# Third layer's heads: two key blocks' value products in a row, score passes interleaved

## The chip, the core and the metric

The kernel runs on one core of a Trainium2 chip. The metric is the device time of one execution in microseconds (us). The core's engines run unsynchronised, each with its own queue: TensorE multiplies matrices (PE in the profile, its weight loads PEld), VectorE (DVE), ScalarE (ACT) and GpSimd (POOL) work on elements, and SyncE (SP) here only issues transfers. Semaphores order them: an instruction adds to one when it is done, and another engine's `wait_ge` holds its queue until the value is there.

## What is computed

Four layers in turn, each `x = x + attention(norm(x)) + feed_forward(norm(x))`, on x of 2 sequences, 1024 tokens and 256 features. The change lies in the third layer's attention (called L2, counted from 0), 16 heads of 16 features:

```
q, k, v = (split_heads(q), split_heads(k), split_heads(v))   # (2, 16, 1024, 16)
scores = jnp.einsum('bhqd,bhkd->bhqk', q, k) * scale
attn = jnp.einsum('bhqk,bhkd->bhqd', jax.nn.softmax(scores, axis=-1), v)
g = jax.nn.sigmoid(gate)
combined = g * mem_out + (1.0 - g) * attn
```

## The kernel before

`l2_heads` computes `attn` in 32 steps, one for each pair (h, b) of head and sequence; step n is n = 2h + b. Steps 0, 1, 30 and 31 are written out, those between are a hardware loop (`steps`, L1565). For each pair the work on TensorE comes in three kinds:

- First pass (`first_pass`, L1647, matmul L1658). Scores with queries on partitions, in NP = 16 pieces of 128 queries by 512 keys. Its only use is the maximum of each row. Piece i goes into PSUM buffer `s1[i % 2]`, and before it is written TensorE waits on `maxed` until VectorE has reduced piece i - 2 (L1657). VectorE does one `reduce_max` of 128x512 for each piece (`maxima`, L1747), and after 16 pieces a small `take_top` (L1752).
- Second pass (`second_pass`, L1661, matmul L1668). Scores with keys on partitions, for one key block kb of 8: two matmuls of 128x512 into `s2[kb % 2]`. The row maxima are subtracted through two extra rows of the contraction. TensorE waits on `exped` until ScalarE has done key block kb - 2; ScalarE takes the exponential of all 1024 queries in one instruction (L1734) into `PT`.
- Value products (`values`, L1672, matmul L1680). For one key block four matmuls of 256 queries each, with a stationary operand 32 columns wide, put side by side in the four column groups of the array (their outputs are the partition groups 0-31, 32-63, 64-95 and 96-127 of `pv`). Each float32 matmul has two records in the trace, so a key block shows as eight.

A fourth piece, `turn` (L1684), comes once a step: it transposes the finished `ctxT` of an earlier step (two transposes, not in steps 0 and 1) and the row maxima `top` of the next one (L1695), and counts up `turned`. On VectorE `split_max` (L1754) waits for it, makes `mhi` and `mlo` (L1758, L1760), and `normalise` (L1762, two instructions, not in steps 0 and 1) follows. SyncE then carries `mhi` and `mlo` into `Q2` (`load_max`, L1615) for the second pass of the next step.

The work is staggered: in step n TensorE does the second pass of n, the first pass of n + 2, and the value products of n - 1. The order is written out by hand in `step` (L1702): for each kb, two second-pass matmuls, two first-pass pieces, at kb == TURN_AT (1) the `turn`, then the value products of kb. VectorE's order (`step`, L1778) is: maxima of pieces 0 to 2 * (TURN_AT + 1) - 1, `split_max`, `normalise`, the other maxima, `take_top`. So TURN_AT sets both TensorE's place for the turn and how many maxima VectorE does ahead of waiting for it.

Step 0 has no value products, and steps 30 and 31 have no first pass. After step 31 the value products of the last pair run as eight key blocks in a row.

Of the kernel before, what the change touches and what calls it, by code (L numbers as in the profile page):

```python
# [21 lines left out]
NQ = S // P  # L22
# [54 lines left out]
def wait(engine, sem, value):  # L77

    if not isinstance(value, int) or value > 0:
        engine.wait_ge(sem, value)  # L80
# [1229 lines left out]
def l2_attn(nc, k, a):  # L1310

    split = nc.dram_tensor("l2_split", [2, 4, D, T], F32, kind="Internal").ap()
    with Stage(nc, "l2a") as st:
        VA = st.sb("VA", [P, TT, L2_HEADS, L2_W])
        mem = st.sb("mem", [P, DC, T])
        gate = st.sb("gate", [P, 2, DC])
        with Stage(nc, "l2q") as s2:
            QF = s2.sb("QF", [P, DC, T])  # L1320
            KF = s2.sb("KF", [P, DC, T])
            hi, lo = s2.sb("hi", [P, 2, DC, BANK], F32R), s2.sb("lo", [P, 2, DC, BANK], F32R)
            hi_stored, lo_stored = [s2.sem(f"hi_stored{i}") for i in range(2)], [s2.sem(f"lo_stored{i}") for i in range(2)]
            l2_project(nc, k, a, split, VA, QF, KF, hi, lo, hi_stored, lo_stored)
            l2_memory(nc, k, a, VA, QF, KF, mem, gate, hi_stored + lo_stored)
        CT = st.sb("CT", [P, TT, D])
        l2_heads(nc, k, split, VA, CT)
        l2_output(nc, k, a, CT, mem, gate)
# [210 lines left out]
def l2_heads(nc, k, split, VA, CT):  # L1539
# [4 lines left out]
    with Stage(nc, "l2h") as st:  # L1544
# [17 lines left out]
        pv_made, pv_kept, turned, inv_ready, ctx_kept = (st.sem(n) for n in ("pv_made", "pv_kept", "turned", "inv_ready", "ctx_kept"))  # L1562
        vh_ready, second_loads = st.sem("vh_ready"), st.sem("second_loads")
        NP = 2 * NQ
        TURN_AT = 1  # L1565
        MROW = SPLIT

        def steps(engine, step):

            for b in range(B):  # L1570
                step(0, b)
            with engine.Fori(1, L2_HEADS - 1) as h:
                for b in range(B):
                    step(h, b)
            for b in range(B):
                step(L2_HEADS - 1, b)

        def after(h, b, n):

            return (h + (b + n) // B, (b + n) % B)  # L1580

        def before(h, b):
            return (h, b - 1) if b else (h - 1, B - 1)

        def is_first(h, b):
            return isinstance(h, int) and h == 0 and b == 0

        def exists(h, b, n):

            return not isinstance(h, int) or B * h + b + n < L2_N  # L1590

        with nc.Block() as block:
# [56 lines left out]
            @block.tensor  # L1649
            def _(pe):  # L1650
                def first_pass(h, b, pieces):
                    n = B * h + b
                    for i in pieces:
                        t, z = divmod(i, 2)
                        if i == 0:
                            pe.wait_ge(q1_loaded[b], 32 * h + 32)
                        wait(pe, maxed, NP * n + i - 1)  # L1657
                        pe.matmul(s1[i % 2][:, :], Q1[:, b, t * P:(t + 1) * P], K1[:, b, z * BANK:(z + 1) * BANK],  # L1658
                                  start=True, stop=True).then_inc(s1_made, 1)

                def second_pass(h, b, kb):  # L1661
                    n = B * h + b
                    if kb == 0:
                        pe.wait_ge(q2_loaded[b], 32 * h + 32)
                        pe.wait_ge(m_loaded[b], 32 * h + 32)
                    wait(pe, exped, NQ * n + kb - 1)
                    for z in range(NZ):
                        mm = pe.matmul(s2[kb % 2][:, z * BANK:(z + 1) * BANK], K2[:, b, kb * P:(kb + 1) * P],  # L1668
                                       Q2[:, b, z * BANK:(z + 1) * BANK], start=True, stop=True)
                    mm.then_inc(s2_made, 1)  # L1670

                def values(h, b, kb):  # L1672

                    n = B * h + b
                    if kb == 0:
                        pe.wait_ge(vh_ready, n + 1)
                        pe.wait_ge(exped, NQ * (n + 1))
                        wait(pe, pv_kept, n)
                    for g in range(4):
                        mm = pe.matmul(pv[g * L2_W:(g + 1) * L2_W, 0:2 * P], VH[:, b, kb, :],  # L1680
                                       PT[:, b, kb, g * 2 * P:(g + 1) * 2 * P], start=(kb == 0), stop=(kb == NQ - 1), skip_group_check=True)
                    if kb == NQ - 1:
                        mm.then_inc(pv_made, 1)

                def turn(m, ctx, top_of):

                    wait(pe, m_ready, min(m, L2_N) if isinstance(m, int) else m)
                    if ctx:
                        pe.wait_ge(pv_kept, m - 2)
                        wait(pe, ctx_kept, m - 3)  # L1690
                        for i in range(2):
                            mm = pe.transpose(turns[:, i * P:(i + 1) * P], ctxT[:, i * P:(i + 1) * P], k.ident[:, :])
                    if top_of is not None:
                        pe.wait_ge(top_ready, m + 1)
                        mm = pe.transpose(pmt, top[:, top_of, :], k.ident[:, :])  # L1695
                    mm.then_inc(turned, 1)

                first_pass(0, 0, range(NP))
                turn(0, False, 0)
                first_pass(0, 1, range(NP))  # L1700

                def step(h, b):  # L1702
                    for kb in range(NQ):
                        second_pass(h, b, kb)
                        if exists(h, b, 2):
                            first_pass(*after(h, b, 2), range(2 * kb, 2 * kb + 2))
                        if kb == TURN_AT:
                            turn(B * h + b + 1, not isinstance(h, int) or h > 0, (b + 1) % B if exists(h, b, 1) else None)
                        if not is_first(h, b):
                            values(*before(h, b), kb)  # L1710

                steps(pe, step)
                turn(L2_N + 1, True, None)
                for kb in range(NQ):
                    values(L2_HEADS - 1, B - 1, kb)
                turn(L2_N + 2, True, None)
# [24 lines left out]
            def _(dve):  # L1741
# [36 lines left out]
                def step(h, b):  # L1778
                    n = B * h + b
                    more = exists(h, b, 2)  # L1780
                    early = 2 * (TURN_AT + 1)
                    if more:
# [995 lines left out]
```

## Time and profile before

| | |
|---|---|
| Time, median of 3 runs | 4075.12 us (4071.56 to 4076.61) |
| Profiled execution | 4091.38 us, span 4089.6 us |
| Span of this stage's heads in it | 2301.2 to 2773.6 us, 472 us |
| Mean granted TensorE clock | 0.929 |
| Busy share: PE, PEld, DVE, ACT, POOL | 89%, 65%, 57%, 39%, 34% |

The whole program has one execution in the trace. What matters for this change is a stretch of 12% of it, in which one step repeats. The trace rows give start and duration of instructions. A matmul's record runs from when its data are first fetched to a modelled end, so the records of neighbours overlap, and their starts tell the pace. A matmul whose weights could be loaded ahead has a record of 0.39 to 0.40 us at full clock; one that had to wait for its weights has one of about 0.50 us, and its data stream some 0.1 us after its record begins.

### The profile page before, as it was taken

How to read it: one execution, taken by the hardware profiler on the slowest of the kernel's cores; microseconds unless marked ns; L12 is line 12 of the kernel's file. 1: busy time of each engine (PE TensorE's matmuls, PEld its weight loads, DVE VectorE, ACT ScalarE, POOL GpSimd, SP SyncE). 2: the span in 40 equal slices, each digit the busy share in tenths (PEclk: the TensorE clock that was granted, in tenths of full speed). 3: DMA queues.
4: the chain of work that ended last, by engine and by line, in shares of the span. 5: the costliest groups of instructions: out<-in, count | busy, mean ns of one | idle time of the engine just before them, and what ended most of it. 6: DMA issues, size and time to landing. Idle time of an engine off the chain costs nothing. (4 is left out here: it accounts for less than half of the span.)

```text
span 4089.6 us, 65022 instructions
## 1 busy us (share of the span) xinstructions
PE 3655.6 (89%) x21096; PEld 2662.2 (65%) x21096; DVE 2325.4 (57%) x4783; ACT 1598.5 (39%) x2884; POOL 1389.7 (34%) x1087
## 2 busy tenths in 40 slices
PE   6999999999797999999966799997899979999676
PEld 4777777777575888888833344443678737776354
DVE  3555555555325566666647778774566646666444
ACT  2444444444233444444423166662333333333211
POOL 1333333333135666666614000000223352334254
PEclk8999999999898999999978799998899989999755
DMA  0000000000001000000004122210333313332144
GB/s 35 5 5 5 3 5 5 5 3 5 32 0 45 18 17 20 18 17 17 8 3 183 42 74 76 76 65 26 83 82 87 90 34 76 91 82 54 57 103 95
DMA packets 115990, 178.66 MB, mean 44 GB/s; under 512 B 22288, under 2 KB 65040, under 8 KB 115600
## 3 DMA queue, kind: packets, MB, share of 16 engines
q1 hardware_dynamic: 109776, 169.38, 13.8%
q0 software_dynamic: 6144, 8.39, 1.3%
q8 instruction: 38, 0.62, 0.1%
q14 instruction: 32, 0.26, 0.0%
HBM read 151.51 MB, written 25.95 MB: 43 GB/s over the span
## 5 line engine op out<-in xcount | busy, mean ns | idle before, releaser
L424 POOL TENSOR_TENSOR l0h_probs<-l0h_probs,l0h_inv 128x128 f32<-128x128 f32 (+7 forms) x256 | 292.8, 1146 | 585.7 <-DVE l0h_inv L459 585.7
L1747 DVE TENSOR_REDUCE l2h_half<-l2h_s 128x1 f32<-128x512 f32 x512 | 329.6, 685 | 94.2 <-PE l2h_s L1658 94.1
L1734 ACT ACTIVATE l2h_PT<-l2h_s 128x1024 f32<-128x1024 f32 x256 | 261.9, 1023 | 194.2 <-PE l2h_s L1668 194.2
L355 PE MATMUL l0h_sc<-l0a_KT,l0h_QT 128*128 x768 | 296.7, 499 | 30.0 <-ACT l0h_probs L528 28.3
L382 PE MATMUL l0h_cx<-l0h_PT,l0h_VG 128*128 128x128 f32 x2304 | 300.7, 276 | 0.0
L528 ACT ACTIVATE l0h_probs<-l0h_sc,l0h_negtop 128x128 f32<-128x128 f32 (+7 forms) x256 | 189.6, 741 | 245.4 <-DVE l0h_negtop L454 245.0
L382 PEld LDWEIGHTS l0h_cx<-l0h_PT,l0h_VG 128*128 128x128 f32 x2304 | 278.0, 192 | 1.1
L159 POOL TENSOR_TENSOR XN<-XN,n_rstd 128x512 f32<-128x512 f32 x32 | 39.8, 1265 | 635.2 <-DVE n_rstd L140 635.2
L2189 DVE TENSOR_TENSOR_SCAN l3p_table<-l3p_decb,l3p_eye 128x512 f32<-128x512 f32 x128 | 149.8, 1212 | 116.0 <-DMA l3p_prow<-l_decays 92.2
L1658 PE MATMUL l2h_s<-l2h_K,l2h_Q 128*128 128x512 f32 x512 | 180.2, 429 | 21.7 <-DMA l2h_K<-l_split 18.0
L452 DVE TENSOR_REDUCE l0h_top<-l0h_sc 128x1 f32<-128x128 f32 (+7 forms) x256 | 194.0, 758 | 8.8
L355 PEld LDWEIGHTS l0h_sc<-l0a_KT,l0h_QT 128*128 128x128 f32 x768 | 125.5, 192 | 106.7 <-issue 63.9
L1668 PE MATMUL l2h_s<-l2h_Q,l2h_K 128*128 128x512 f32 x512 | 187.5, 447 | 0.1
L391 PE MATMUL l0h_outp<-l0h_ctxT,l0h_wd 128*128 128x128 f32 x1024 | 163.8, 283 | 24.8 <-ACT l0h_ctxT L521 11.7
L369 PEld LDWEIGHTS l0h_tp<-ident,l0h_probs 128*128 128x128 f32 x1152 | 138.6, 141 | 64.3 <-issue 39.6
L2157 POOL TENSOR_TENSOR l3p_w_lo<-l3p_w,l3p_w_hi 128x1024 fp32r<-128x1024 f32 x34 | 80.3, 2362 | 276.8 <-ACT l3p_w_hi L2111 276.8
L2147 POOL TENSOR_TENSOR l3a_Y<-l3p_skip,l3p_sz 128x512 f32 (+1 forms) x64 | 81.4, 1272 | 261.6 <-DVE l3p_skip L2180 261.6
L369 PE MATMUL l0h_tp<-ident,l0h_probs 128*128 128x128 f32 x1152 | 168.7, 274 | 0.0
L470 DVE COPY l0h_PT<-l0h_tp 128x256 f32<-128x256 f32 (+2 forms) x192 | 98.6, 514 | 114.2 <-PE l0h_tp L369 112.3
L391 PEld LDWEIGHTS l0h_outp<-l0h_ctxT,l0h_wd 128*128 128x128 f32 x1024 | 134.2, 191 | 44.6 <-ACT l0h_ctxT L521 31.2
L514 ACT ACTIVATE l0h_PT<-l0h_tp 128x512 f32<-128x512 f32 (+1 forms) x192 | 100.8, 525 | 159.5 <-PE l0h_tp L369 159.1
L1680 PE MATMUL l2h_pv<-l2h_PT,l2h_VH 128*32 128x256 f32 x2048 | 162.1, 391 | 0.2 <-ACT l2h_ctxT L1725 0.2
(410 smaller groups left out, 9081.1 us busy)
## 6 DMA issues: line engine op xcount, KB each, us to landing
l3p_decb<-l_decays SPq DMA_DIRECT2D x128, 256.0 KB, 5.2
l3p_w<-L_w SPq DMA_DIRECT2D x34, 512.0 KB, 5.9
l2h_Q<-l_split SPq DMA_DIRECT2D x64, 256.0 KB
l2h_K<-l_split SPq DMA_DIRECT2D x64, 256.0 KB
l3p_prow<-l_decays SPq DMA_DIRECT2D x128, 128.0 KB, 5.6
l_split<-l2q_hi SPq DMA_DIRECT2D x16, 512.0 KB, 4.0
l_split<-l2q_lo SPq DMA_DIRECT2D x16, 512.0 KB, 3.8
mx_wgu<-L_ffn_w_gate_up SPq DMA_DIRECT2D x32, 256.0 KB
```

The lines of the kernel that those rows point to most:

```text
L355: mm = pe.matmul(sc[u % 2][:, lo:lo + n], QT[:, u * P:(u + 1) * P], KT[:, ds(g, 1), b * S + lo:b * S + lo + n], start=True, stop=True)
L369: mm = pe.transpose(tp[n % 2][:, (kb - q) * P:(kb - q + 1) * P], probs[:, u % 4, kb * P:(kb + 1) * P], k.ident[:, :])
L382: mm = pe.matmul(cx[:, 0:P], VG[:, b * NQ + kb, :], PT[:, u % 2, kb, :], start=(kb == 0), stop=(kb == t))
L391: mm = pe.matmul(outp[:, c * P:(c + 1) * P], wd[:, c * P:(c + 1) * P], ctxT[:, u % 2, :], start=True, stop=True)
L424: pool.tensor_tensor(p, p, inv[:, u % 4:u % 4 + 1].to_broadcast([P, keys(u)]), ALU.mult).then_inc(probs_scaled, 1)
L452: dve.reduce_max(top[:, u % 2:u % 2 + 1], sc[u % 2][:, 0:keys(u)], AX_X).then_inc(top_ready, 1)
L528: act.activation(probs[:, u % 4, 0:keys(u)], sc[u % 2][:, 0:keys(u)], ACT.Exp, bias=negtop[:, u % 2:u % 2 + 1], scale=L0_SCALE, accum_out= ...
L1658: pe.matmul(s1[i % 2][:, :], Q1[:, b, t * P:(t + 1) * P], K1[:, b, z * BANK:(z + 1) * BANK], start=True, stop=True).then_inc(s1_made, 1)
L1668: mm = pe.matmul(s2[kb % 2][:, z * BANK:(z + 1) * BANK], K2[:, b, kb * P:(kb + 1) * P], Q2[:, b, z * BANK:(z + 1) * BANK], start=True, sto ...
L1680: mm = pe.matmul(pv[g * L2_W:(g + 1) * L2_W, 0:2 * P], VH[:, b, kb, :], PT[:, b, kb, g * 2 * P:(g + 1) * 2 * P], start=(kb == 0), stop=(kb ...
L1734: act.activation(PT[:, b, kb, :], s2[kb % 2][:, :], ACT.Exp, scale=L2_SCALE).then_inc(exped, 1)
L1747: dve.reduce_max(half[:, b, t, z:z + 1], s1[i % 2][:, :], AX_X).then_inc(maxed, 1)
```

## The change

In `step` of TensorE the loop runs over pairs of key blocks (kb = 0, 2, 4, 6). For each pair: piece 2kb of the first pass, the second pass of kb, piece 2kb + 1, the second pass of kb + 1, pieces 2kb + 2 and 2kb + 3, the turn where kb is TURN_AT, and then the value products of kb and kb + 1 in a row. TURN_AT goes from 1 to 2, so the turn comes after piece 7, and VectorE does maxima 0 to 5 ahead of it. No instruction is added or removed. Buffers, waits, transfers and the code of the other engines stay as they are.

```diff
-        TURN_AT = 1
+        TURN_AT = 2
@@ step of TensorE
-                    for kb in range(NQ):
-                        second_pass(h, b, kb)
+                    for kb in range(0, NQ, 2):
+                        for i in range(2):
+                            if exists(h, b, 2):
+                                first_pass(*after(h, b, 2), (2 * kb + i,))
+                            second_pass(h, b, kb + i)
                         if exists(h, b, 2):
-                            first_pass(*after(h, b, 2), range(2 * kb, 2 * kb + 2))
+                            first_pass(*after(h, b, 2), (2 * kb + 2, 2 * kb + 3))
                         if kb == TURN_AT:
                             turn(B * h + b + 1, not isinstance(h, int) or h > 0, (b + 1) % B if exists(h, b, 1) else None)
                         if not is_first(h, b):
-                            values(*before(h, b), kb)
+                            for i in range(2):
+                                values(*before(h, b), kb + i)
```

## Rows read from the trace of the kernel before

**Rows 1.** The page: TensorE's busy share, and VectorE's group of maxima.

```profile
PE 3655.6 (89%) x21096; PEld 2662.2 (65%) x21096; DVE 2325.4 (57%) x4783; ACT 1598.5 (39%) x2884; POOL 1389.7 (34%) x1087
...
L1747 DVE TENSOR_REDUCE l2h_half<-l2h_s 128x1 f32<-128x512 f32 x512 | 329.6, 685 | 94.2 <-PE l2h_s L1658 94.1
```

**Rows 2.** Busy time by stretch: ramp, step 0, steps 1-29, steps 30-31.

```profile
core 0: us, PE busy (x) PEld busy (x) DVE busy (x) ACT busy (x) POOL busy (x), PEclk, DMA share, GB/s
2301.20:2326.99 25.79, 21.80 (x34) 9.34 (x35) 20.33 (x34) 0.00 (x0) 0.00 (x0) 0.50 0.18 66
2328.50:2339.40 10.90, 10.22 (x33) 5.55 (x32) 10.42 (x18) 8.03 (x9) 0.00 (x0) 0.93 0.17 66
2339.40:2748.00 408.60, 408.44 (x2873) 200.62 (x2876) 326.39 (x609) 254.60 (x291) 0.00 (x0) 1.00 0.20 74
2748.00:2773.20 25.20, 23.64 (x229) 9.70 (x228) 1.99 (x9) 17.50 (x21) 0.00 (x0) 1.00 0.07 22
```

**Rows 3.** Timeline, one key block; start us, us, engine, line, xcount, [idle before].

```profile
2503.79 0.64 PE L1680 MATMUL l2h_pv<-l2h_PT,l2h_VH 128*32 128x256 f32 x8
2504.36 0.30 PEld L1668 LDWEIGHTS l2h_s<-l2h_Q,l2h_K 128*128 128x128 f32 x2 [0.41 <-issue]
2504.36 0.74 PE L1668 MATMUL l2h_s<-l2h_Q,l2h_K 128*128 128x512 f32 x2
...
2504.94 0.63 PE L1658 MATMUL l2h_s<-l2h_K,l2h_Q 128*128 128x512 f32 x2
2505.13 1.02 ACT L1734 ACTIVATE l2h_PT<-l2h_s 128x1024 f32<-128x1024 f32 x1 [0.68 <-PE l2h_s L1668]
2505.37 0.69 DVE L1747 TENSOR_REDUCE l2h_half<-l2h_s 128x1 f32<-128x512 f32 x1 [0.41 <-PE l2h_s L1658]
...
2505.49 0.64 PE L1680 MATMUL l2h_pv<-l2h_PT,l2h_VH 128*32 128x256 f32 x8
```

**Rows 4.** Timeline, ScalarE's first exponential of steps 2 and 29.

```profile
2353.48 1.01 ACT L1734 ACTIVATE l2h_PT<-l2h_s 128x1024 f32<-128x1024 f32 x1
...
2733.97 1.02 ACT L1734 ACTIVATE l2h_PT<-l2h_s 128x1024 f32<-128x1024 f32 x1
```

**Rows 5.** Timeline, PE and DVE, around one turn and the two blocks behind.

```profile
2510.04 0.62 PE L1658 MATMUL l2h_s<-l2h_K,l2h_Q 128*128 128x512 f32 x2
...
2510.72 0.27 PE L1695 MATMUL l2h_turns<-ident,l2h_top 128*8 128x128 f32 x1
...
2510.92 0.64 PE L1680 MATMUL l2h_pv<-l2h_PT,l2h_VH 128*32 128x256 f32 x8
...
2511.67 0.27 DVE L1758 CAST l2h_mhi<-l2h_turns 8x128 fp32r<-8x128 f32 x1
...
2512.51 0.29 DVE L1769 TENSOR_TENSOR l2a_CT<-l2h_turns,l2h_inv 128x128 f32 x1
...
2512.72 1.28 DVE L1747 TENSOR_REDUCE l2h_half<-l2h_s 128x1 f32<-128x512 f32 x2
...
2513.75 0.81 PE L1658 MATMUL l2h_s<-l2h_K,l2h_Q 128*128 128x512 f32 x2
...
2514.05 0.19 PEld L1658 LDWEIGHTS l2h_s<-l2h_K,l2h_Q 128*128 128x128 f32 x1 [0.34 <-DVE l2h_half L1747]
...
2514.49 0.64 PE L1680 MATMUL l2h_pv<-l2h_PT,l2h_VH 128*32 128x256 f32 x8
```

**Rows 6.** Timeline, last value products: eight key blocks in a row.

```profile
2769.10 3.66 PE L1680 MATMUL l2h_pv<-l2h_PT,l2h_VH 128*32 128x256 f32 x64
```

**Rows 7.** Timeline of step 0, no value products: the split, then first and second pass.

```profile
2331.42 0.27 DVE L1758 CAST l2h_mhi<-l2h_turns 8x128 fp32r<-8x128 f32 x1
...
2331.93 0.67 DVE L1747 TENSOR_REDUCE l2h_half<-l2h_s 128x1 f32<-128x512 f32 x1
...
2334.25 1.02 ACT L1734 ACTIVATE l2h_PT<-l2h_s 128x1024 f32<-128x1024 f32 x1 [0.68 <-PE l2h_s L1668]
2334.53 0.19 PEld L1658 LDWEIGHTS l2h_s<-l2h_K,l2h_Q 128*128 128x128 f32 x1 [0.41 <-DVE l2h_half L1747]
...
2335.54 1.03 ACT L1734 ACTIVATE l2h_PT<-l2h_s 128x1024 f32<-128x1024 f32 x1 [0.26 <-PE l2h_s L1668]
```

**Rows 8.** Timeline of step 30, no first pass: end of the turn, then exponentials.

```profile
2749.26 0.27 PE L1695 MATMUL l2h_turns<-ident,l2h_top 128*8 128x128 f32 x1
...
2749.57 0.28 DVE L1758 CAST l2h_mhi<-l2h_turns 8x128 fp32r<-8x128 f32 x1 [1.54 <-PE l2h_turns L1695]
...
2752.03 1.02 ACT L1734 ACTIVATE l2h_PT<-l2h_s 128x1024 f32<-128x1024 f32 x1 [0.21 <-PE l2h_s L1668]
...
2753.26 1.02 ACT L1734 ACTIVATE l2h_PT<-l2h_s 128x1024 f32<-128x1024 f32 x1 [0.21 <-PE l2h_s L1668]
```

**Rows 9.** SyncE's waits in steps 1 to 29: us in total, times, longest us.

```profile
SPq L1608 <- PE l2h_s L1668: 195.1, 28, 7.2
SPq L1615 <- DVE l2h_mlo L1760: 59.0, 28, 3.0
```

## The prediction

> **What bounds the kernel now.** I read the page first: TensorE is busy 89% of the span, but VectorE's largest group of instructions, the maxima of this stage, stands there too [rows 1]. Then the stage alone, by stretch. In steps 1 to 29 TensorE is busy 408.4 of 408.6 us at full clock (1.00, which is 2.4 GHz), VectorE 326.4 and ScalarE 254.6 [rows 2]. So TensorE sets the pace on average, with VectorE at 80% behind it. The busy time of TensorE is made of overlapping records, so the pace must be read from starts.
>
> One key block [rows 3]: the value products start at 2503.79, the second pass at 2504.36, the first pass at 2504.94, the next value products at 2505.49: 1.70 us. Its parts:
> - value products, up to the weight load of the second pass: 0.57;
> - from that load to the second matmul of the pair: 0.74 less a record of 0.40 = 0.34. Where weights were loaded ahead, matmuls start 0.63 - 0.40 = 0.23 apart (0.24 where the operands change), so 0.10 of the 0.34 is an exposed load;
> - second matmul to first piece 0.24, to second piece 0.23;
> - last piece (2504.94 + 0.23 = 2505.17) to the value products at 2505.49: 0.32, where the next score matmul would have come after 0.23.
>
> Sum 0.57 + 0.34 + 0.47 + 0.32 = 1.70. The stream of four groups side by side needs about 0.43 for a key block: eight in a row take 3.66 from first start to last end, one takes 0.64, and (3.66 - 0.64) / 7 = 0.43 [rows 6]. So a visit to the value products costs 0.57 + 0.10 + 0.09 = 0.76, and each further key block in the same visit 0.43.
>
> A step, from the first exponentials of steps 2 and 29, is (2733.97 - 2353.48) / 27 = 14.09 us [rows 4]. Eight times 1.70 is 13.60. The turn adds 0.33: from the last piece (2510.04 + 0.23 = 2510.27) to the value products at 2510.92 it is 0.65 in place of 0.32 [rows 5]. The last 0.16 is the one wait on VectorE that TensorE feels: the two pieces of kb = 3 take 0.81 in place of 0.62, the load between them released by a maximum, because VectorE came late from the split [rows 5].
>
> **The change, part by part.**
>
> *Value products in pairs.* One visit fewer in each pair: 0.76 - 0.43 = 0.33 us saved. Without any new wait a pair would take 2 x 1.70 - 0.33 = 3.07 us. What stands against it is not in that sum: the order of the score passes.
>
> *First-pass pieces closer together.* There are two s1 buffers, so piece i + 2 waits for the maximum of piece i. The round trip: start of a piece to its maximum 2505.37 - 2504.94 = 0.43 [rows 3]; the maximum 0.69 (mean 0.685) [rows 1]; its end to the released weight load 2514.05 - (2512.72 + 1.28) = 0.05; and that load is exposed, 0.12, since the value products come 0.44 after it and not 0.32 [rows 5]. Sum 1.29 us. Step 0, which has no value products, shows it directly: exponentials 2335.54 - 2334.25 = 1.29 apart, with the piece's load waiting on the maxima [rows 7]. Before, pieces i and i + 2 are a key block, 1.70, apart, so it is hidden. In the new order (call the pieces of a pair F0 to F3) it is F0 S S F1 S S F2 F3 V V. F0 to F2 is six spacings, 1.41: hidden. F1 to F3 is four spacings, 0.24 + 0.23 + 0.24 + 0.23 = 0.94: F3 waits 1.29 - 0.94 = 0.35 us in every pair. F2 to the next F0 is over 2 us: hidden. VectorE is not behind from elsewhere: F3's maximum ends 0.43 + 0.69 = 1.12 after F3 starts, and the value products take TensorE 0.32 + 1.00 + 0.10 = 1.42 to the next F0. So a pair takes 3.07 + 0.35 = 3.42 us, against 3.40: the wait eats what the pairing saves. Bounds for the wait: 0.33 to 0.36 by the spread of the same rows (round trip 1.28 to 1.29, spacing 0.93 to 0.95).
>
> *The turn after piece 7, and six maxima ahead of it.* Before, VectorE is still at a maximum when the turn is done (2510.72 + 0.27 = 2510.99) and starts the split at 2511.67, with no idle time [rows 5]. After, VectorE has done maximum 5 when piece 7 is allowed to start (that is what piece 7 waits for), so it idles until the turn is done, and maxima 6 and 7 queue behind split and normalise though their scores are there. From the start of piece 7: turn done 0.45 + 0.27 = 0.72; split starts 0.04 later (2749.57 against 2749.26 + 0.27) [rows 8]; split and normalise hold VectorE 2512.72 - 2511.67 = 1.05 [rows 5]; maximum 6 takes 0.69; release 0.05. Piece 8 can load at 0.76 + 1.05 + 0.69 + 0.05 = 2.55 us. TensorE gets to it after the turn 0.65 and two key blocks of value products 0.57 + 0.43: at 1.65 us. The wait is 0.90 us once a step, bounds 0.85 to 0.95. It replaces the 0.16 of before. Behind it everything on TensorE is queued; piece 9 no longer waits, since maximum 7 ends 0.6 after maximum 6.
>
> *Work moved past other queues.* SyncE's `load_max` waits for the split, now about 3 us later in the step. SyncE waits there 59 us in 28 steps now, and 195 us (up to 7.2 each) at the next second-pass load, L1608 [rows 9]: the later start comes out of that. The `mhi` and `mlo` are wanted at the next step, some 8 us after the split. ScalarE gets two exponentials closer together: second-pass pairs are 0.70 apart, an exponential takes 1.02 [rows 3], both fit into 3.42 us and `s2` has two buffers, free again a pair later. Cost nothing, while ScalarE's 2.05 of 3.42 holds.
>
> *A step:* 4 x 3.42 + 0.33 + 0.90 = 14.91 us, against 14.09: + 0.82. For steps 2 to 29: 28 x 0.82 = + 23.0.
> *Edges.* Step 1 has value products but neither normalise nor the ctxT transposes: the split starts 0.23 + 0.27 + 0.04 = 0.54 after piece 7 and alone holds VectorE 2331.93 - 2331.42 = 0.51 [rows 7]. Load of piece 8 at 0.54 + 0.51 + 0.69 + 0.05 = 1.79 against 0.43 + 1.00: wait 0.36, + 0.3 net. Step 0 has no value products to cover the same 1.79 (they were bound by the round trip already): + 1.0. Steps 30 and 31 have no maxima: a key block takes 2753.26 - 2752.03 = 1.23 [rows 8], a pair 2.46; after, 2.13 by TensorE, but two exponentials in a row make it up to 2.41; I take 2.25: 8 x 0.21 = - 1.7.
> **Sum:** 23.0 + 0.3 + 1.0 - 1.7 = + 22.6 us. On the profiled execution's span, 4089.6, this gives 4112.2; that execution ran 0.4% above the median (4091.4 against 4075.1), so I put the same difference on the median: 4097.7.
>
> **A rule that says otherwise.** The load for the second pass begins 0.57 after the value products [rows 3], though a key block of them streams in 0.43 [rows 6], and going back costs 0.09. The Trainium skill, TensorEngine Tiling (Array Packing), Key Properties, says that changing the tiling mode drains TensorE. The trace agrees: 0.33 us a visit beyond the stream, with the exposed load. By that rule alone, with half the changes gone, the time would be that of rival 1.
>
> **Rivals.**
> 1. *The visits decide, the waits are not felt* (faster). Place: F3 and piece 8. A step would be 4 x 3.07 + 0.33 = 12.61, - 1.48 from 14.09; 29 x - 1.48 - 1.7 = - 45 us: 4030. It needs a round trip under 0.94, or a split that is done by 1.65. For it: 0.1 us gaps on both sides of each visit. Against it: the 1.29 measured in step 0. Chance 0.05.
> 2. *The turn's wait is covered, F3's is not* (no change). A step of 4 x 3.42 + 0.33 = 14.01; 29 x - 0.08 - 1.7 = - 4: 4071. It needs VectorE to take maximum 6 ahead of the split or the chain to be under 1.65 where I have 2.55. Against it: VectorE's order is fixed in its queue. Chance 0.08.
> 3. *The clock falls* (much slower). TensorE would stand 0.9 us once and 0.35 us four times a step. In the ramp it stood and worked in turn and had 0.50, 1.2 GHz; step 0 with its waits on VectorE held 0.93 [rows 2]. At the lower level the streams of a pair double, from 3.42 to about 5.7: + 9 us a step, over 4200 if it stayed so. Chance 0.03.
>
> **How the numbers follow.** Forecast 0.82, rivals 0.05, 0.08 and 0.03, something between forecast and 2 (a shorter turn's wait) 0.02. The bounds, 0.02 x 4 and 0.05 x 1 a step, give 0.13 x 29 = 4 us; small costs where passes alternate (0.02 in a few places a step) 3 us; and the runs of before spread by 5 us. Alone that is 4088 to 4107; to hold 8 in 10, with 0.16 in other cases, I take 4082 to 4110. About 0.2% (8 us) can be told from no change. Slower by more than that: 0.82 + 0.03 + 0.02, less 0.01 for a case between forecast and 2 that falls short of it, 0.86; within: 0.08 + 0.01 = 0.09; faster: 0.05.
>
> **What would show it.** Right: in a step of 14.9 us, piece loads that idle before them by VectorE's maxima in each pair, VectorE idle about 0.9 before the split, put down to the turn, TensorE idle about 0.9 before piece 8, and value products of 1.07 us (x16). Exponentials stand in twos, a step 14.9 apart. Wrong: if F3's load follows F2's at once, the round trip is shorter than I read; if VectorE shows no idle time before the split, the turn's cost is not there; if the clock row in the stage is under 1.00, rival 3.

## The result, and the profile after

| | before | after |
|---|---|---|
| Time, median | 4075.86 us (4071.56 to 4077.09, 4 runs) | 4098.66 us (4098.38 to 4108.7, 4 runs) |
| Profiled execution | 4091.38 us | 4098.61 us |
| A step (first exponentials of steps 2 and 29, over 27) | 14.09 us | 14.95 us |
| Ratio of the runs | | 1.0064, 95% interval 1.0046 to 1.0081 |

The change makes the kernel slower by 22.8 us, 0.6%. The forecast was + 22.6 us, 4097.7. The interval of the ratio is + 19 to + 33 us, so the runs fix the size no closer than that.

The length of a step is read from the first exponentials of steps 2 and 29: [rows 4] has those of before, and these are those of after:

```profile
2347.81 1.03 ACT L1738 ACTIVATE l2h_PT<-l2h_s 128x1024 f32<-128x1024 f32 x1
...
2751.39 1.03 ACT L1738 ACTIVATE l2h_PT<-l2h_s 128x1024 f32<-128x1024 f32 x1
```

The spans of the two profiled executions differ by 7.2 us only, because the one of before was long elsewhere: it reaches this stage 8 us later (2289.1 against 2280.9), and its last stage, the experts, is 9 us longer, on code that is the same. The stage itself shows the whole difference. Its busy time by stretch, after: the ramp, step 0, steps 1 to 29, steps 30 and 31, with the columns of [rows 2]:

```profile
core 0: us, PE busy (x) PEld busy (x) DVE busy (x) ACT busy (x) POOL busy (x), PEclk, DMA share, GB/s
2293.20:2320.60 27.40, 23.21 (x37) 10.05 (x37) 22.14 (x37) 0.00 (x0) 0.00 (x0) 0.50 0.18 70
2320.60:2333.70 13.10, 10.71 (x34) 6.53 (x34) 10.90 (x19) 8.17 (x9) 0.00 (x0) 0.87 0.13 48
2333.70:2766.10 432.40, 395.92 (x2869) 220.75 (x2869) 339.09 (x607) 244.92 (x290) 0.00 (x0) 1.00 0.19 70
2766.10:2791.00 24.90, 22.72 (x237) 11.36 (x237) 2.46 (x10) 16.67 (x21) 0.00 (x0) 1.00 0.06 21
```

The clock is 1.00 from step 1 on, as before. In steps 1 to 29 TensorE was busy 408.4 of 408.6 us [rows 2] and is now busy 395.9 of 432.4 on the same work: 36 us without any matmul record have appeared. VectorE's busy time reads 339.1 (326.4 before): its instructions take no longer, but fewer of their records overlap, 0.61 us apart and 0.69 long where they follow one another.

Where it stands still is in the groups of instructions of steps 2 to 28 (L1658 is the first pass, L1751 `reduce_max`, L1762 the first instruction of the split; busy, mean ns, then idle time before the group and what ended it):

```profile
L1658 PE MATMUL l2h_s<-l2h_K,l2h_Q 128*128 128x512 f32 x433 | 192.6, 445 | 34.6 <-DVE l2h_half L1751 25.0
...
L1658 PEld LDWEIGHTS l2h_s<-l2h_K,l2h_Q 128*128 128x128 f32 x432 | 80.6, 187 | 137.9 <-DVE l2h_half L1751 126.3
...
L1762 DVE CAST l2h_mhi<-l2h_turns 8x128 fp32r<-8x128 f32 x27 | 7.5, 279 | 27.3 <-PE l2h_turns L1695 27.3
```

The weight loads for the first pass idle 126.3 us until a maximum, in 27 steps. Not all of that is lost: ahead of F0, the first piece of a pair, they idle 0.41 us while the value products still stream (2507.86 below). The matmuls themselves (first row) stood 34.6 us, 25.0 of them until a maximum, 0.93 in each step: that is piece 8. VectorE idles 27.3 us ahead of the split for the turn, 1.01 us a step in the mean; before it idled 0.0 us there in the same group of instructions, as [rows 5] show for one step.

A pair of key blocks without the turn, after, timeline as in [rows 3]:

```profile
2506.86 1.07 PE L1680 MATMUL l2h_pv<-l2h_PT,l2h_VH 128*32 128x256 f32 x16
2507.86 0.19 PEld L1658 LDWEIGHTS l2h_s<-l2h_K,l2h_Q 128*128 128x128 f32 x1 [0.41 <-DVE l2h_half L1751]
...
2508.19 0.63 PE L1668 MATMUL l2h_s<-l2h_Q,l2h_K 128*128 128x512 f32 x2
...
2508.66 0.39 PE L1658 MATMUL l2h_s<-l2h_K,l2h_Q 128*128 128x512 f32 x1
...
2508.89 0.62 PE L1668 MATMUL l2h_s<-l2h_Q,l2h_K 128*128 128x512 f32 x2
...
2509.35 0.98 PE L1658 MATMUL l2h_s<-l2h_K,l2h_Q 128*128 128x512 f32 x2
...
2509.83 0.19 PEld L1658 LDWEIGHTS l2h_s<-l2h_K,l2h_Q 128*128 128x128 f32 x1 [0.51 <-DVE l2h_half L1751]
...
2510.26 1.07 PE L1680 MATMUL l2h_pv<-l2h_PT,l2h_VH 128*32 128x256 f32 x16
```

From one pair of value products to the next it is 2510.26 - 2506.86 = 3.40 us: the forecast was 3.42. Two key blocks of value products take 1.07 where one takes 0.64, so 0.43 for the second. The order is F0 (2507.86), S S, F1 (2508.66), S S, F2 (2509.35) and F3, whose load comes at 2509.83 and was released by a maximum after 0.51 us of idling. It leads to a stream at 2509.83 + 0.11 = 2509.94, which is 1.28 after F1: the round trip. Behind F2 it could have streamed at 2509.35 + 0.23 = 2509.58, so F3 waited 0.36. And the turn, after (compare [rows 5]):

```profile
2501.22 0.98 PE L1658 MATMUL l2h_s<-l2h_K,l2h_Q 128*128 128x512 f32 x2
...
2502.25 0.27 PE L1695 MATMUL l2h_turns<-ident,l2h_top 128*8 128x128 f32 x1
...
2502.46 1.07 PE L1680 MATMUL l2h_pv<-l2h_PT,l2h_VH 128*32 128x256 f32 x16
2502.66 0.28 DVE L1762 CAST l2h_mhi<-l2h_turns 8x128 fp32r<-8x128 f32 x1 [1.01 <-PE l2h_turns L1695]
...
2503.72 1.28 DVE L1751 TENSOR_REDUCE l2h_half<-l2h_s 128x1 f32<-128x512 f32 x2
...
2504.45 0.19 PEld L1658 LDWEIGHTS l2h_s<-l2h_K,l2h_Q 128*128 128x128 f32 x1 [1.41 <-DVE l2h_half L1751]
```

The turn is done at 2502.25 + 0.27 = 2502.52, VectorE has idled 1.01 us for it and starts the split at 2502.66. Maximum 6 starts at 2503.72, 1.06 later, ends at 2504.40, and at 2504.45 piece 8 is loaded. The value products' two key blocks were through at 2502.46 + 1.00 = 2503.46: TensorE waited 0.99 us.

### The profile page after: what moved, and what is told of

It reads as the page before. It is cut to its first block and busy times, and to the rows that moved or that the text cites. A ratio compares the mean times of both kernels' runs of the same rounds, so it can differ in the third digit from the quotient of the medians.

```text
span 4096.8 us, 65022 instructions
## 1 busy us (share of the span) xinstructions
PE 3630.2 (89%) x21096; PEld 2676.5 (65%) x21096; DVE 2336.2 (57%) x4783; ACT 1588.4 (39%) x2884; POOL 1376.2 (34%) x1087
## 5 line engine op out<-in xcount | busy, mean ns | idle before, releaser
L1751 DVE TENSOR_REDUCE l2h_half<-l2h_s 128x1 f32<-128x512 f32 x512 | 340.7, 688 | 76.1 <-PE l2h_s L1658 75.2
L1738 ACT ACTIVATE l2h_PT<-l2h_s 128x1024 f32<-128x1024 f32 x256 | 248.4, 1022 | 212.7 <-PE l2h_s L1668 210.0
L1658 PE MATMUL l2h_s<-l2h_K,l2h_Q 128*128 128x512 f32 x512 | 236.5, 469 | 60.5 <-DVE l2h_half L1751 31.5
L1658 PEld LDWEIGHTS l2h_s<-l2h_K,l2h_Q 128*128 128x128 f32 x512 | 99.2, 194 | 187.9 <-DVE l2h_half L1751 154.3
L1668 PE MATMUL l2h_s<-l2h_Q,l2h_K 128*128 128x512 f32 x512 | 161.7, 399 | 0.0
```

What stands on the lines that cost most here:

```text
L1738: act.activation(PT[:, b, kb, :], s2[kb % 2][:, :], ACT.Exp, scale=L2_SCALE).then_inc(exped, 1)
L1751: dve.reduce_max(half[:, b, t, z:z + 1], s1[i % 2][:, :], AX_X).then_inc(maxed, 1)
```

## The experiments

Eight kernels, in two sets of four, each set on one chip beside the kernel before. The clearest measure is the length of a step in each profile, from the first exponential of step 2 to that of step 29, over 27. Each step has been worked out before its kernel ran ("said ahead"). The kernel before took 4083.9 us on the one chip and 4076.6 on the other, and the expectations count their times from 4075.9, so compare a time with the one in brackets beside it. e2, e4, e5, e6 and e8 have one run each; 15 and 9 runs of the kernel before spread by 14 and 10 us, so for these five the step is the evidence and not the time.

| kernel | score order, pieces ahead of the split | step, us | said ahead | time, us (before on the same chip) |
|---|---|---|---|---|
| before | S S F0 F1 V, 4 | 14.09 | | |
| after | F0 S S F1 S S F2 F3 V V, 6 | 14.95 | 14.91 | 4098.7 (4075.9) |
| e1_eight_maxima | as after, 8 | 13.97 | 13.95 | 4079.1 (4083.9) |
| e2_pairs_old_scores | S S F0 F1 S S F2 F3 V V, 8 | 15.44 | 15.5 | 4120.2 (4083.9) |
| e3_two_pieces_first | F0 F1 S S S S F2 F3 V V, 8 | 13.57 | 13.7 | 4067.2 (4083.9) |
| e4_normalise_later | as after, 6 | 14.78 | 14.8 | 4101.7 (4083.9) |
| e5_turn_moved_alone | as before, 6 | 14.12 | 14.1 | 4077.2 (4076.6) |
| e6_interleaved_alone | F0 S S F1 V, 4 | 13.90 | 13.96 | 4069.6 (4076.6) |
| e7_turn_between_pieces | as e3 with two edits, 8 | 13.34 | 13.3 | 4054.9 (4076.6) |
| e8_four_blocks | four key blocks, 8 | 14.24 | 14.1 | 4080.7 (4076.6) |

The theory is the one of the prediction: value products in pairs save 0.33 us a visit; the two s1 buffers have a round trip of 1.29 us; and once a step VectorE idles for the turn with two maxima behind the split. Rival A puts the loss on TensorE itself: the visits or the alternation of the two score passes. The others are told where they stand.

**e1_eight_maxima: the turn's wait by itself.** From the changed kernel:

```diff
-                    early = 2 * (TURN_AT + 1)
+                    early = 2 * TURN_AT + 4
```

> The changed kernel with one edit: VectorE does eight maxima of a step, not six, ahead of the split. The turn on TensorE stays behind piece 7. My theory (the change loses about 1.0 us a step because VectorE stands idle until the turn is done and keeps maxima 6 and 7 behind split and normalise): VectorE has maxima 6 and 7 to do while the turn runs, its idle time before the split goes from 1.0 us to nothing, piece 8 no longer waits, a step goes from 14.95 to 4 x 3.41 + 0.33 = 13.95 us, the whole time to 4098.7 - 29 = about 4069 us. Rival A (the loss is TensorE's own: a visit of two key blocks to the value products and back, or alternating the two score passes, costs more than the rows said, and the waits on VectorE are only where it shows): the step stays within 0.2 us of 14.95 and the time near 4095.

The step fell by 0.98 us to 13.97. The time is no longer above before: a ratio of 0.999, interval 0.998 to 1.0, which can't be told from no change. Its timeline at a turn, after piece 7:

```profile
2480.89 2.68 DVE L1751 TENSOR_REDUCE l2h_half<-l2h_s 128x1 f32<-128x512 f32 x4 [0.72 <-PE l2h_s L1658]
...
2482.89 0.27 PE L1695 MATMUL l2h_turns<-ident,l2h_top 128*8 128x128 f32 x1
...
2483.10 1.07 PE L1680 MATMUL l2h_pv<-l2h_PT,l2h_VH 128*32 128x256 f32 x16
2483.49 0.27 DVE L1762 CAST l2h_mhi<-l2h_turns 8x128 fp32r<-8x128 f32 x1
...
2484.10 0.19 PEld L1658 LDWEIGHTS l2h_s<-l2h_K,l2h_Q 128*128 128x128 f32 x1 [0.41 <-issue]
...
2484.64 2.08 DVE L1751 TENSOR_REDUCE l2h_half<-l2h_s 128x1 f32<-128x512 f32 x3
```

The split starts at 2483.49 with no idle time ahead of it, since maxima 6 and 7 ran while the turn was made (x4 from 2480.89). Piece 8 is loaded at 2484.10, 1.00 after the value products began: TensorE comes to it without waiting. Rival A falls: nothing of TensorE's order was touched.

**e4_normalise_later: is only the chain to piece 8 to blame?** From the changed kernel, VectorE's order in a step:

```diff
                     if exists(h, b, 1):
                         split_max(*after(h, b, 1))
+                    if more:
+                        maxima(*after(h, b, 2), range(early, early + 2))
                     if not isinstance(h, int) or h > 0:
                         normalise(h - 1, b)
                     if more:
-                        maxima(*after(h, b, 2), range(early, NP))
+                        maxima(*after(h, b, 2), range(early + 2, NP))
```

> The changed kernel with one edit: VectorE does split, maxima 6 and 7, then normalise (before, split, normalise, maxima 6 and 7). It takes 0.54 us out of the chain from the turn to piece 8 and puts it behind maximum 7. My theory: piece 8's wait falls from 1.0 to about 0.46, but VectorE then comes 0.4 late to maximum 8 and piece 10 waits that long: a step of about 14.8 us in place of 14.95, so little is won, 4094 us. Rival B (the wait of piece 8 is the only place where VectorE's order counts in the turn): the whole 0.54 comes back, a step of 14.4 us, about 4083.

The step is 14.78, so 0.17 us were won. Piece 8 comes 0.55 us sooner after the turn, and 0.38 of that is lost at the next place:

```profile
2488.68 1.07 PE L1680 MATMUL l2h_pv<-l2h_PT,l2h_VH 128*32 128x256 f32 x16
2488.88 0.28 DVE L1762 CAST l2h_mhi<-l2h_turns 8x128 fp32r<-8x128 f32 x1 [1.01 <-PE l2h_turns L1695]
...
2489.40 1.27 DVE L1751 TENSOR_REDUCE l2h_half<-l2h_s 128x1 f32<-128x512 f32 x2
...
2490.12 0.19 PEld L1658 LDWEIGHTS l2h_s<-l2h_K,l2h_Q 128*128 128x128 f32 x1 [0.85 <-DVE l2h_half L1751]
...
2490.59 0.18 DVE L1771 RECIPROCAL l2h_inv<-l2h_turns 128x8 f32<-128x8 f32 x1
...
2491.13 2.57 DVE L1751 TENSOR_REDUCE l2h_half<-l2h_s 128x1 f32<-128x512 f32 x4
...
2491.86 0.19 PEld L1658 LDWEIGHTS l2h_s<-l2h_K,l2h_Q 128*128 128x128 f32 x1 [0.52 <-DVE l2h_half L1751]
```

The split still idled 1.01 us for the turn. Piece 8 is loaded at 2490.12, 1.44 after the value products began (1.99 in the changed kernel). But normalise now runs from 2490.59 on, maximum 8 starts at 2491.13 instead of about 2490.66, and piece 10 waits at 2491.86, where the changed kernel has no wait. Rival B falls: VectorE's idle time has to go, not one instruction out of a chain.

**e2_pairs_old_scores and e3_two_pieces_first: the s1 buffers.** Both from the kernel of e1, in `step` of TensorE:

```diff
@@ e2_pairs_old_scores
-                        for i in range(2):
-                            if exists(h, b, 2):
-                                first_pass(*after(h, b, 2), (2 * kb + i,))
-                            second_pass(h, b, kb + i)
+                        second_pass(h, b, kb)
+                        if exists(h, b, 2):
+                            first_pass(*after(h, b, 2), (2 * kb, 2 * kb + 1))
+                        second_pass(h, b, kb + 1)
@@ e3_two_pieces_first
-                        for i in range(2):
-                            if exists(h, b, 2):
-                                first_pass(*after(h, b, 2), (2 * kb + i,))
-                            second_pass(h, b, kb + i)
+                        if exists(h, b, 2):
+                            first_pass(*after(h, b, 2), (2 * kb, 2 * kb + 1))
+                        for i in range(2):
+                            second_pass(h, b, kb + i)
```

> Value products in pairs and eight maxima ahead of the split, but the score passes in the old order: S S F0 F1 S S F2 F3 V V (S a second-pass matmul, F a first-pass piece, V the value products of a key block). My theory (one round trip of 1.29 us for each of two s1 buffers, and maxima at least 0.61 us apart): F2 waits 1.29 - 0.94 = 0.35, F3 comes no earlier than 0.43 + 0.61 + 0.69 + 0.17 = 1.90 after F0, which is 0.38 more, so 0.73 in a pair where the changed kernel has 0.35: a pair 3.79, a step 4 x 3.79 + 0.33 = 15.5 us, the whole time about 4114 us. Rival A (alternating the passes costs, not the buffers): this order alternates less, so its step is no longer than with the interleaved order and eight maxima, 13.95 us, about 4069.

> Value products in pairs and eight maxima ahead of the split, and the score passes in the order F0 F1 S S S S F2 F3 V V. My theory: F2 comes 1.41 after F0, above the round trip of 1.29; F3 no earlier than 0.43 + 0.61 + 0.69 + 0.17 = 1.90 after F0, where it could come at 1.65: a wait of 0.25 in a pair and not 0.35. A pair 3.31, and about 0.13 once a step from the split: a step of 13.7 us, the whole time 4075.9 - 29 x 0.39 - 2.6 (steps 30 and 31) = about 4062 us, faster than both kernels. Rival A: pieces one behind the other make TensorE wait on VectorE as before, so no better than F0 S S F1 S S F2 F3, a step of 13.95 or more and about 4069.

The same instructions in three orders give steps of 13.97, 15.44 and 13.57 us, within 0.13 us of the steps that one round trip and one pace of the maxima had said. e2, the last pair of a step:

```profile
2500.63 0.63 PE L1658 MATMUL l2h_s<-l2h_K,l2h_Q 128*128 128x512 f32 x2
...
2501.10 0.62 PE L1668 MATMUL l2h_s<-l2h_Q,l2h_K 128*128 128x512 f32 x2
2501.81 0.19 PEld L1658 LDWEIGHTS l2h_s<-l2h_K,l2h_Q 128*128 128x128 f32 x1 [0.52 <-DVE l2h_half L1751]
...
2502.41 0.19 PEld L1658 LDWEIGHTS l2h_s<-l2h_K,l2h_Q 128*128 128x128 f32 x1 [0.41 <-DVE l2h_half L1751]
...
2502.84 1.07 PE L1680 MATMUL l2h_pv<-l2h_PT,l2h_VH 128*32 128x256 f32 x16
```

F2 is loaded at 2501.81 and F3 at 2502.41, each released by a maximum, and they stream 0.11 later. Unhindered, F2 would stream 0.24 after the last second-pass matmul (2501.10 + 0.23), at 2501.57: a wait of 0.35. F3 would stream 0.23 after F2, at 2502.15: 0.37. e3, the last pair of a step:

```profile
2483.76 0.39 PE L1658 MATMUL l2h_s<-l2h_K,l2h_Q 128*128 128x512 f32 x1
2483.96 2.67 DVE L1751 TENSOR_REDUCE l2h_half<-l2h_s 128x1 f32<-128x512 f32 x4 [0.62 <-PE l2h_s L1658]
2483.99 1.09 PE L1668 MATMUL l2h_s<-l2h_Q,l2h_K 128*128 128x512 f32 x4
...
2484.92 0.88 PE L1658 MATMUL l2h_s<-l2h_K,l2h_Q 128*128 128x512 f32 x2
2485.30 0.19 PEld L1658 LDWEIGHTS l2h_s<-l2h_K,l2h_Q 128*128 128x128 f32 x1 [0.41 <-DVE l2h_half L1751]
```

Only F3 waits: it streams at 2485.30 + 0.11 = 2485.41, and 0.23 after F2 would be 2485.15, a wait of 0.26. e3 was the first kernel clearly below before: ratio 0.9958, interval 0.9944 to 0.9972. Its step is 0.13 shorter than I had said: I had counted a second small wait behind the split, and the profile has none; by the exponentials the pair with the turn is 0.34 longer than the others, the turn itself.

**e5_turn_moved_alone and e6_interleaved_alone: one part of the change alone.** Both from the kernel before:

```diff
@@ e5_turn_moved_alone
-        TURN_AT = 1
+        TURN_AT = 2
@@ e6_interleaved_alone
-                        second_pass(h, b, kb)
                         if exists(h, b, 2):
-                            first_pass(*after(h, b, 2), range(2 * kb, 2 * kb + 2))
+                            first_pass(*after(h, b, 2), (2 * kb,))
+                        second_pass(h, b, kb)
+                        if exists(h, b, 2):
+                            first_pass(*after(h, b, 2), (2 * kb + 1,))
```

> The kernel before with TURN_AT = 2 alone: the turn after piece 5, six maxima ahead of the split, value products one key block at a time. My theory: VectorE's maxima 4 and 5 stand right behind each other, it is still at the second when the turn is done, so it never idles ahead of the split, as before: a step of 14.1 us and no difference from before. The turn's wait in the changed kernel comes from the later turn together with pieces 6 and 7 sent ahead of it. Rival C (the later turn is enough by itself): a step of 14.9 us, + 24 us.

> The kernel before with the score passes alone interleaved: F0 S S F1 V for each key block, TURN_AT = 1. No piece comes nearer than 1.70 us to the one two ahead of it, so no wait of the s1 buffers; the one wait behind the split (0.16) falls to about 0.03, since the pieces come evenly. My theory: a key block stays 1.70 us, a step 8 x 1.70 + 0.33 + 0.03 = 13.96 us, about 4 us less than before. Rival A (alternating the passes costs TensorE time of its own): a key block over 1.75, a step over 14.4, + 9 us or more.

e5 leaves the step at 14.12 (14.09), so the later turn costs nothing by itself: rival C falls. (One of its steps took 15.12, with TensorE idle for 0.98 us at the landing of a transfer of `mlo`; the other 26 took 14.06 to 14.13.) e6 has a step of 13.90. The one time of e6, 7 us under before, fits 29 x 0.19 = 5.5, but is less than the 10 us over which runs of one kernel spread there. The alternation of the passes costs nothing (against rival A); the 0.19 us won are about the 0.16 that before waited behind its split. So two of the three parts of the change are harmless or good alone. The third, the pairing, was in no run by itself. What costs comes with it, in two parts: F3's wait takes back what the visits save (e1, 13.97 against 14.09), and pieces 6 and 7 ahead of the turn with their maxima behind it cost the other 0.98 us, which e1 gives back.

**e8_four_blocks: more of the pairing.** From the kernel of e1, with groups of four key blocks:

```diff
-                    for kb in range(0, NQ, 2):
+                    for kb in range(0, NQ, 4):
...
+                        second_pass(h, b, kb)
+                        for i in range(1, 4):
+                            second_pass(h, b, kb + i)
+                            if exists(h, b, 2):
+                                first_pass(*after(h, b, 2), (2 * kb + 2 * i, 2 * kb + 2 * i + 1))
...
-                            for i in range(2):
+                            for i in range(4):
                                 values(*before(h, b), kb + i)
```

> Four key blocks' value products in a row: F0 F1 S S S S F2 F3 S S F4 F5 S S F6 F7 V V V V, twice a step, the turn after piece 7, eight maxima ahead of the split. It saves two more visits a step (0.66 us), but eight pieces must pass two s1 buffers between two visits: F7 comes no earlier than 1.90 + 2 x 1.29 + 0.1 = 4.6 us after F0, where TensorE could be there at 3.5. My theory: four key blocks take 4.59 + 0.32 + 0.57 + 3 x 0.43 + 0.10 = 6.9 us, a step 14.1 us, half a microsecond more than the order in pairs (13.57) though it has half the visits; about 4075 us. Rival A (visits are what costs): a step of 13.57 - 0.66 = 12.9 us, about 4045.

A step has 14.24 us: half the visits of e3, and 0.67 us longer (0.14 of it more than I had worked out). The working had left out ScalarE: by the trace the second-pass loads idle at an exponential twice a step, 0.24 us each time (13.2 us, 54 times in steps 2 to 28), at the third key block of each four. No run separates how much of the 0.14 that makes. This is the cleanest answer to rival A: the visits can be saved, but between two of them eight pieces must pass the two s1 buffers; in each half of a step their eight maxima run in one unbroken row of about 5.35 us.

**e7_turn_between_pieces: a version that beats both.** From the kernel of e3: the turn stands between pieces 6 and 7, and normalise after maximum 11.

```diff
@@ step of TensorE
                         if exists(h, b, 2):
-                            first_pass(*after(h, b, 2), (2 * kb + 2, 2 * kb + 3))
+                            first_pass(*after(h, b, 2), (2 * kb + 2,))
                         if kb == TURN_AT:
                             turn(B * h + b + 1, not isinstance(h, int) or h > 0, (b + 1) % B if exists(h, b, 1) else None)
+                        if exists(h, b, 2):
+                            first_pass(*after(h, b, 2), (2 * kb + 3,))
@@ step of VectorE
                     if exists(h, b, 1):
                         split_max(*after(h, b, 1))
+                    if more:
+                        maxima(*after(h, b, 2), range(early, early + 4))
                     if not isinstance(h, int) or h > 0:
                         normalise(h - 1, b)
                     if more:
-                        maxima(*after(h, b, 2), range(early, NP))
+                        maxima(*after(h, b, 2), range(early + 4, NP))
```

> The fastest order so far (F0 F1 S S S S F2 F3 V V, eight maxima ahead of the split; a step of 13.57 us) with two more edits: the turn stands between pieces 6 and 7, where TensorE waits 0.25 us on VectorE anyway, and normalise comes after maximum 11, into the idle time that VectorE has behind every fourth maximum. My theory: the turn's 0.33 us fill that wait, piece 7 starts at about 1.97 after piece 4 in place of 1.89, the value products follow it at once, and a step falls by 0.25 to about 13.3 us: 29 x 0.25 = 7 us less than that order, a ratio to before of about 0.994. Rival B (VectorE's split still comes late to maximum 8 and the next pair gives the gain back): a step of 13.5 or more, no gain beyond 0.996.

```profile
2475.41 0.39 PE L1658 MATMUL l2h_s<-l2h_K,l2h_Q 128*128 128x512 f32 x1
...
2475.86 0.27 PE L1695 MATMUL l2h_turns<-ident,l2h_top 128*8 128x128 f32 x1
...
2475.89 0.48 PE L1658 MATMUL l2h_s<-l2h_K,l2h_Q 128*128 128x512 f32 x1
...
2476.30 1.07 PE L1680 MATMUL l2h_pv<-l2h_PT,l2h_VH 128*32 128x256 f32 x16
2477.05 0.27 DVE L1764 CAST l2h_mhi<-l2h_turns 8x128 fp32r<-8x128 f32 x1
```

Piece 7 starts at 2475.89, right behind the transposes and with no wait on a maximum, and the value products follow at 2476.30. The step is 13.34 us and the time 4054.9 us against 4076.6: a ratio of 0.9942, interval 0.9929 to 0.9956, 0.6% faster than the kernel before where the change was 0.6% slower, with the same instructions. Rival B of its expectation falls. The kernel has two edits over e3, and how the 0.23 us divide between the turn's place and the later normalise was not measured. (One of its steps took 14.08, with TensorE idle for 0.53 us at the landing of a transfer of `K`; the median step is 13.32.)

## Why the prediction was right

- *What bounds the stage.* Right: in the changed kernel and in e1 to e7 the steps moved with waits between TensorE and VectorE, through two buffers and one turn. In e8 ScalarE had a part as well.
- *The pairing saves 0.33 us a visit.* Right, and seen apart from the waits in steps 30 and 31, which have no first pass: a pair took 2.46 before [rows 8] and takes 2.13 after, both times at full clock:

```profile
2766.12 1.94 ACT L1738 ACTIVATE l2h_PT<-l2h_s 128x1024 f32<-128x1024 f32 x2
2768.25 1.94 ACT L1738 ACTIVATE l2h_PT<-l2h_s 128x1024 f32<-128x1024 f32 x2 [0.19 <-PE l2h_s L1668]
```

- *F3 waits 0.35 us in every pair.* Right, 0.36 in the pair shown: a pair 3.40 against 3.42 said and 3.40 before; e2 and e3 moved it as the round trip says.
- *The turn's wait, 0.90 us.* The mechanism was right, the size short: 0.99. The missing 0.1 is one term, the start of the split after the turn. I took 0.04 from [rows 8], which is step 30; in the loop it is 0.13.
- *The step, + 0.82.* It is + 0.86: 0.1 more at the turn, 4 x 0.015 less in the pairs. Over steps 2 to 28, from first exponential to first exponential (2347.81 to 2751.39 after), it is 403.58 - 380.49 = 23.1 us and step 29 adds 0.7, so + 23.8 where I had + 23.0.
- *Edges.* Each was off, and that they nearly cancel is luck. Step 1 is as long as before (14.08 against 14.07; I said + 0.3): the wait behind its turn came as said, but the kernel before had lost 0.37 at the start of the same step (2.06 us between its first two exponentials, 1.68 in step 2), and that went. Step 0 grew by 1.8 us (I said + 1.0 in all). Of that 1.2 is the turn's wait, since with eight maxima, in e1, the step is 1.2 shorter; the other 0.6 I had not costed, and the granted clock of the stretch, 0.87 against 0.93, may be part of it. And the first exponential comes 1.0 later in the stage: the first piece of pair 2 is now ahead of the first second-pass matmul and waits on the maxima of the pieces before it, in the ramp, at a clock of 0.50. I had not costed that either. The other kernels bear it out: from the stage's first load to the first exponential it is 26.9 us before and in e2, which begin with S S, and 27.9 after, in e1 and in e6, which begin with F0. Steps 30 and 31 gave back 2.4 us, not 1.7: I had feared that two exponentials in a row would hold TensorE, but two take 1.94 us and not 2.05, under the 2.13 of a pair.
- *The sum.* From the first first-pass matmul to the end of the last normalise the stage grew from 473.1 to 497.3 us in the profiles, 24.2; the whole kernel by 22.8 in the medians, and + 22.6 was said. The parts differ by up to 1.8 us from what was said, and the interval is 14 us wide: that the total is met within 0.2 us is luck. What was foreseen is the sign, the place of the two waits and their size within 0.1 us.
- *The rivals.* Rival 1 (the visits decide) is refuted by the changed kernel, whose step is 14.95 and not 12.61, and by e8 and e2. Rival 2 (the turn's wait is covered) describes e1, which had to be built for it. Rival 3 (the clock falls) did not come: 1.00 through steps 1 to 29, though TensorE stands still up to 0.93 us at a time.
- *The rule of the Trainium skill on tiling modes* (TensorEngine Tiling (Array Packing), Key Properties). The trace agrees with it in so far as each visit costs 0.33 us beyond its stream, before and after; 0.10 of that is a load that isn't hidden, and no run separates what of the rest is a drain. The rule pointed rightly at what the pairing is worth, and says nothing of what it costs here. Fewer changes of mode paid here only as far as the buffers between two changes let the rest of the work through: e8.

## What to carry to other kernels

Before moving work together on the engine that sets the pace, measure the round trip of each buffer pair around it (start of the producer, consumer, release, next start), and lay the new order against it: a distance below the round trip can give the whole gain back, as here 0.35 us too little gave back the 0.33 of a visit. Where an engine without much time to spare (here VectorE, busy 80%) waits for one event in a fixed queue, put ahead of the wait whatever is already there to be done, and place the event early enough; here that one number (eight maxima, not six) was worth 1 us of 15. And a wait that can't be avoided is a place for work that must be done anyway, as the turn between pieces 6 and 7 (e7, where it came together with the later normalise).

## What the runs showed beside that

VectorE, idle at the wait for the turn, starts later in the hardware loop than in the steps written out. In the changed kernel, between the end of the turn's last record and the split it was 0.04 us in the written-out steps (0, 1 and 30) and 0.13 to 0.14 in all 28 of the loop; in the loop a register operation of VectorE's sequencer, 0.05 us long, stands between the two, at the line of the waits. That it is the cause is likely and was not tested. The difference is 0.1 us a step; where VectorE was still at a maximum when the turn was done, as in e1, the split began with no idle time at all. And exponentials in a row overlap by 0.1 us: two take 1.94, one 1.02.
